# The last step of six layer norms moved from VectorE to ScalarE, in a two-layer decoder pipeline on one core

## The reference, cut to what matters

```
def _layernorm(x, axis=-1, eps=1e-05):
    m = jnp.mean(x, axis=axis, keepdims=True)
    v = jnp.var(x, axis=axis, keepdims=True)
    return (x - m) / jnp.sqrt(v + eps)

x = _layernorm(x + L0_attn(x))          # norm 1
x = _layernorm(x + L0_xattn(x, ctx))    # norm 2
x = _layernorm(x + L0_ffn(x))           # norm 3
x = _layernorm(x + L1_attn(x))          # norm 4, the scan
x = _layernorm(x + L1_xattn(x, ctx))    # norm 5
x = _layernorm(x + L1_ffn(x))           # norm 6, the experts
```

## Time and profile before

| | us |
|---|---|
| median of 3 runs | 3486.57 |
| lowest and highest | 3484.23, 3490.03 |
| the profiled execution's own time | 3486.94 |
| its span, first to last instruction | 3485.1 |
| TensorE matmuls busy | 2634.2 |
| VectorE busy | 2650.8 |
| ScalarE busy | 1564.4 |
| GpSimd busy | 1610.6 |

### The profile page before, as it was taken

How to read it: one execution, slowest core, us unless ns; L and a number is a source line. 1 busy time by engine, 2 the same in 40 slices (tenths; PEclk the granted TensorE clock), 3 DMA queues, 4 the chain that set the end, 5 groups by cost and what they waited for, 6 DMA issues and landing times.

```text
span 3485.1 us, 41835 instructions
## 1 busy us (share of the span) xinstructions
PE 2634.2 (76%) x10956; PEld 1505.0 (43%) x10956; DVE 2650.8 (76%) x4314; ACT 1564.4 (45%) x2838; POOL 1610.6 (46%) x1223
## 2 busy tenths in 40 slices
PE   5876878787786887768787786877778787777746
PEld 3434435354443544435354443544445353443413
DVE  2287887968789687887968789696877968788693
ACT  1364544535345453544535445453544545354430
POOL 1064461735537263562735437262562726447180
PEclk8868788887888878888887888888788887888877
DMA  3000000000000000000000000000000000000000
GB/s 115 0 16 0 21 1 27 0 22 6 0 27 0 27 0 7 21 0 27 0 22 6 0 27 0 27 0 13 15 0 27 0 22 6 0 12 0 12 0 12
DMA packets 16786, 45.63 MB, mean 13 GB/s; under 512 B 2376, under 2 KB 6992, under 8 KB 16336
## 3 DMA queue, kind: packets, MB, share of 16 engines
q1 hardware_dynamic: 16592, 43.90, 3.5%
HBM read 35.50 MB, written 8.39 MB: 13 GB/s over the span
## 4 chain that ended last, share of the span: by engine, by line
PE 37%; DVE 28%; issue 19%; ACT 9%; POOL 4%; DVEq 2%; SPq 0%; DMA 0%; ACTq 0%; POOLq 0%
PE bank L487 35%; DVE h_ring L1010 10%; POOL ysum L1537 4%; DVE x L392 3%; DVE x L1107 2%; PE bank L400 2%; DVE smax L915 2%; DVE soft L990 2%; ACT a_ring L1372 1%; DVE ln_stats L374 1%; DVE xpad L1016 1%; ACT soft L1349 1%; DVE qT L965 1%; ACT bank L1367 1%; ACT kmask L1312 1%
## 5 line engine op out<-in xcount | busy, mean ns | idle before, releaser
L1537 POOL TENSOR_TENSOR ysum<-ysum,h_ring 128x512 f32<-128x512 f32 x896 | 1152.4, 1286 | 476.5 <-DVE h_ring L1010 411.2
L1010 DVE TENSOR_TENSOR_SCAN h_ring<-a_ring,bank 128x512 f32<-128x512 f32 x1024 | 1170.9, 1199 | 103.2 <-ACT a_ring L1372 50.8
L487 PE MATMUL bank<-w_expert_w,x45T 128*128 128x512 f32 x1024 | 607.8, 732 | 226.2 <-DVE x L1107 224.6
L1372 ACT ACTIVATE a_ring<-soft,decay 128x510 f32<-128x510 f32 x1024 | 666.7, 715 | 141.7 <-DVE h_ring L1010 140.2
L1513 POOL TENSOR_TENSOR kmask<-kT,w_columns 128x960 f32<-128x960 f32 x64 | 115.5, 1838 | 753.8 <-ACT kT L1260 753.8
L487 PEld LDWEIGHTS bank<-w_expert_w,x45T 128*128 128x128 f32 x1024 | 212.3, 224 | 501.4 <-DVE x L1107 276.2
L1282 ACT ACTIVATE probs<-bank 120x512 f32<-120x512 f32 x256 | 138.3, 593 | 411.8 <-PE bank L487 411.8
L487 PE MATMUL bank<-kmask,w_cn_w 128*128 128x256 f32 (+2 forms) x768 | 277.3, 470 | 44.1 <-ACT kmask L1316 20.3
L400 PE MATMUL bank<-w_ident,x 128*128 128x128 f32 x640 | 136.8, 350 | 224.9 <-DVE x L392 224.9
L1107 DVE SCALAR_TENSOR_TENSOR x<-bank,weight,x 128x256 f32<-128x256 f32 x512 | 212.0, 471 | 72.0 <-PE bank L487 72.0
L962 DVE TENSOR_SCALAR kmask<-kmask,gate_scale,base 128x256 f32<-128x256 f32 x96 | 40.3, 420 | 278.7 <-ACT kmask L1326 278.7
(11 more groups left out here) (144 smaller groups left out, 3879.8 us busy)
## 6 DMA issues: line engine op xcount, KB each, us to landing
x0T<-in_xT SPq DMA_DIRECT2D x16, 512.0 KB, 3.2
x<-in_x SPq DMA_DIRECT2D x16, 512.0 KB, 4.2
out<-x SPq DMA_DIRECT2D x16, 512.0 KB, 3.1
ctxT<-in_ctxT SPq DMA_DIRECT2D x16, 240.0 KB, 4.3
ctxTb<-in_ctxT SPq DMA_DIRECT2D x16, 240.0 KB, 2.6
ctxb<-in_ctx SPq DMA_DIRECT2D x16, 240.0 KB, 3.1
w_expert_w<-in_expert_w SPq DMA_DIRECT2D x1, 2048.0 KB
w_winT<-in_winT SPq DMA_DIRECT2D x1, 1024.0 KB
```

What stands on the lines that cost most here:

```text
L487: return pe.matmul(o, l, r, start=start, stop=stop)
L1010: scanned.then(v.tensor_tensor_scan(h_ring[:, k % HRING, :], a_ring[:, k % RING, :, :].rearrange("p b s -> p (b s)"), xc2, 0.0, ALU.mult, ...
L1372: a.activation(a_ring[:, k % RING, :, 1:S], delta[:, c, :].rearrange("p (b s) -> p b s", b=NB)[:, :, 1:S], ACT.Exp, scale=decay[:, k:k + 1 ...
L1537: p.tensor_tensor(out=total, in0=first, in1=h_ring[:, k % HRING, :], op=ALU.add)\
```

## The change

The apply of all six norms becomes one ScalarE activation for each tile: Identity with scale rstd and bias shift, where shift = -mean x rstd. VectorE makes the shift of all four tiles in one instruction (`norm_shift`, 128x4) in the place where its applies stood, and signals it; ScalarE's four activations stand right behind the norm's rstd (`norm_apply`). For norm 6 VectorE's instruction moves from the end of the turn to between norm 4's and norm 3's sum. Tiles, transposes, copies and all other instructions stay.

```diff
--- before.py
+++ after.py
@@ -251,6 +251,7 @@
                 self.mv = sb(f"{name}_mv", [P, NT, 2])
                 self.logv = sb(f"{name}_logv", [P, NT])
                 self.rstd = sb(f"{name}_rstd", [P, NT])
+                self.shift = sb(f"{name}_shift", [P, NT])
                 self.x = x
                 self.sum = x if sum_ is None else sum_
                 self.xT = xT
@@ -259,6 +260,7 @@
                 self.var_ready = sem(f"{name}_var_ready", 1)
                 self.log_ready = sem(f"{name}_log_ready", 1)
                 self.rstd_ready = sem(f"{name}_rstd_ready", 1)
+                self.shift_ready = sem(f"{name}_shift_ready", 1)
                 self.x_ready = sem(f"{name}_x_ready", NT)
                 if xT is not None:
                     self.turned = sem(f"{name}_turned", DC)
@@ -386,11 +388,16 @@
             a.wait_ge(n.log_ready.sem, n.log_ready.at(g, 1))
             a.activation(n.rstd[:, :], n.logv[:, :], ACT.Exp, scale=-0.5).then_inc(n.rstd_ready.sem, 1)
 
-        def norm_apply(v, n, g):
+        def norm_shift(v, n, g):
             v.wait_ge(n.rstd_ready.sem, n.rstd_ready.at(g, 1))
+            v.scalar_tensor_tensor(out=n.shift[:, :], in0=n.mv[:, :, 0], scalar=-1.0, in1=n.rstd[:, :],
+                                   op0=ALU.mult, op1=ALU.mult).then_inc(n.shift_ready.sem, 1)
+
+        def norm_apply(a, n, g):
+            a.wait_ge(n.shift_ready.sem, n.shift_ready.at(g, 1))
             for t in range(NT):
-                v.tensor_scalar(n.x[:, t, :], n.sum[:, t, :], n.mv[:, t, 0:1], n.rstd[:, t:t + 1],
-                                ALU.subtract, ALU.mult).then_inc(n.x_ready.sem, 1)
+                a.activation(n.x[:, t, :], n.sum[:, t, :], ACT.Identity, bias=n.shift[:, t:t + 1],
+                             scale=n.rstd[:, t:t + 1]).then_inc(n.x_ready.sem, 1)
 
         def norm_turn(pe, n, g, banks):
 
@@ -1121,18 +1128,11 @@
                 last.then_inc(n.var_ready.sem, 1)
                 n.chain.end()
 
-            def ln6_apply(g):
-                n = n6
-                v.wait_ge(n.rstd_ready.sem, n.rstd_ready.at(g, 1))
-                for t in range(NT):
-                    v.tensor_scalar(n.x[:, t, :], acc[:, t, :], n.mv[:, t, 0:1], n.rstd[:, t:t + 1],
-                                    ALU.subtract, ALU.mult).then_inc(n.x_ready.sem, 1)
-
             def turn_(f, m, b):
 
                 if f is not None:
                     ln1_sum(f)
-                    norm_apply(v, n1, f)
+                    norm_shift(v, n1, f)
                 if b is not None:
                     gated(b)
                 if f is not None:
@@ -1144,7 +1144,7 @@
                 if f is not None:
                     maxima(f, 0, 2)
                 if b is not None:
-                    norm_apply(v, n5, b)
+                    norm_shift(v, n5, b)
                 states(m, 1)
                 if f is not None:
                     maxima(f, 2, 3)
@@ -1194,7 +1194,7 @@
                     ln2_sum(f)
                 states(m, 53)
                 if f is not None:
-                    norm_apply(v, n2, f)
+                    norm_shift(v, n2, f)
                 if b is not None:
                     combine(b, 12, 14)
                 states(m, 58)
@@ -1213,13 +1213,13 @@
                     if m is not None and s == CYC - 2:
                         ln4_sum(m)
                 if m is not None:
-                    norm_apply(v, n4, m)
+                    norm_shift(v, n4, m)
+                if b is not None:
+                    norm_shift(v, n6, b)
                 if f is not None:
                     ln3_sum(f)
                 if f is not None:
-                    norm_apply(v, n3, f)
-                if b is not None:
-                    ln6_apply(b)
+                    norm_shift(v, n3, f)
 
             scanned.n = None
             setup()
@@ -1398,10 +1398,12 @@
                     feat(f, 1)
                 if m is not None:
                     norm_rstd(a, n3, m)
+                    norm_apply(a, n3, m)
                 if b is not None:
                     norm_copy(a, n4, b, MB)
                 if f is not None:
                     norm_rstd(a, n1, f)
+                    norm_apply(a, n1, f)
                 if b is not None:
                     gated(b)
                 if m is not None:
@@ -1422,6 +1424,7 @@
                     softplus(m)
                 if b is not None:
                     norm_rstd(a, n5, b)
+                    norm_apply(a, n5, b)
                     norm_copy(a, n5, b, MB)
                 decays(m, 6)
                 if b is not None:
@@ -1441,6 +1444,7 @@
                 decays(m, 54)
                 if f is not None:
                     norm_rstd(a, n2, f)
+                    norm_apply(a, n2, f)
                 decays(m, 56)
                 if f is not None:
                     copy_and_sum(f)
@@ -1464,8 +1468,10 @@
                     nat()
                 if m is not None:
                     norm_rstd(a, n4, m)
+                    norm_apply(a, n4, m)
                 if b is not None:
                     norm_rstd(a, n6, b)
+                    norm_apply(a, n6, b)
 
             setup()
             turn_(0, None, None)
```

## The result

| | before | after |
|---|---|---|
| median of 4 runs each, us | 3485.40 (3482.41 to 3490.03) | 3546.23 (3540.93 to 3550.92) |
| ratio | | 1.0176, 95% interval 1.0163 to 1.0189 |
| span of the profiled execution, us | 3485.1 | 3539.1 |

The change makes the kernel slower by 1.8%: 61 us between the medians, 54 between the two profiled executions (the one of after is the shortest of its four). The forecast was 3518, 32 us slower, with a range up to 3552: the sign and the range hold, but the forecast size is little more than half of the measured one, and the forecast's own narrower range (3500 to 3540) misses it.

A forecast was written before the change was run, and what follows sets the result against it. No engine is full; waits between engines bound the kernel. Seam 13 x 3.43 less norm 5 and norm 2 14 x 1.84 gives +18.8 us, edges +13, together +32: 3518 us, own range 3500 to 3540, 8-in-10 range 3472 to 3552.

The forecast's parts named there:

- The rival of cheaper applies: All ScalarE applies: two per-partition operands cost as one, four applies take 1.70 us, kernel 3497; chance 0.10.
- The seam: Between two turns: norms 4, 6 and 1 on ScalarE delay the table load and TensorE by 3.43 us, 13 times.
- the norm-1 sum: VectorE behind its loop branch at the seam: first norm-1 sum starts 1.15 us later, because the resume stands bare.
- Norm 5: Within each turn: shift held by one GpSimd addition, then ScalarE applies; 1.76 us gained, bounds 2.6 and 0.5.
- Norm 2: Behind a VectorE scan: last output 1526.60 against 1526.68, so nothing; decays held up are hidden by four expert additions.
- Outside the loop: First turns, the turn behind the loop and the last one: norms' handoffs and applies add +13 us together.
- the sum: Whole loop: 13 seams of +3.43 us less 14 turns of 1.84 us make +18.8 us.
- Both clock rivals: TensorE's clock falls at the norm-3 projections (3563, chance 0.10) or returns early at norm 5 (3465, chance 0.14).
- The rival at the seam: Norm-3 projections: longer wait lowers TensorE's clock, about 3.5 us 13 times, +45 us, 3563; chance 0.10.
- a sign that the prediction named as wrong: TensorE: a granted clock that falls before the norm-3 projections would show the forecast wrong.
- The rival in which the clock makes it faster: Norm 5: transposes end 1.8 us sooner and 2.4 GHz returns at once, 3.8 us a turn, 3465; chance 0.14.
- C: Theory put to the follow-up runs: TensorE's granted clock decides what a turn keeps of a gain or loss.

The follow-up runs named there:

- the last kernel: Kernel before with norms 2 and 5 applied on ScalarE, plus 28 identity transposes and three more in each gap between norm 5's first four transposes: 3435.26 us.
- the fuller fillers: Kernel before with norm 5 on ScalarE, 28 identity transposes on TensorE and three more in each gap between norm 5's first four transposes: 3435.77 us.
- both delays: Kernel before with three, or thirteen, small ScalarE Identity instructions ahead of the gate's first Gelu in every turn: 3491.64 us and 3530.21 us.
- the changed kernel with fillers: Changed kernel with 28 identity transposes on TensorE ahead of norm 5's transposes: 3491.84 us, ratio 1.0017 to before.
- with more: Kernel before with 28 identity transposes and six more in each gap between norm 5's first four transposes: 3490.04 us, ratio 1.0013.

## Why the prediction was right, and where it was short

**The apply.** Estimated 591 ns and 2.04 us for four; the rows have 589 ns (x320 and x64) and 2.07. The estimate worked out from the Trainium skill (ScalarE: Activation LUTs, What ACT_TABLE_LOAD costs) was 2.06; with two pointer operands the trace now agrees. The rival of cheaper applies is out.

**The seam.** Forecast +3.43 us to the table load, measured +2.77. The features came as worked out (+3.9 for +4.1, the second's end +1.5 for +1.7), and so did norm 1's handoff and applies: from its second sum to the table load 3.11 us became 5.41, +2.30 for the forecast +2.28. The piece that was too large is the norm-1 sum, +0.5 for +1.15: VectorE's resume behind its branch took 2.75 to 2.99 us in the 13 seams of after (2.8 in the rows above), where the 13 of before have 3.29 to 3.52. The resume was carried over as a constant, and it isn't one. The applies in flight at the branch don't explain it: with norms 2 and 5 on ScalarE and the fillers, VectorE has the same eight applies ahead of its branch as before and its resume takes 2.77 to 3.12 us. The cause stays open.

**Norm 5.** Shift held by one GpSimd addition, applies on ScalarE: forecast 1.76 us gained, measured 2.77 - 0.92 = 1.85. **Norm 2:** nothing, forecast, and shown by the last kernel. **Outside the loop:** +7 us for a forecast +13.

**The step that failed is the sum** "13 x 3.43 - 14 x 1.84 = +18.8 us". Its terms were right within 0.7 us, and they make 2.77 - 1.85 = 0.92 us a turn, 12 us in 13 turns; the loop took 47. The other 2.7 us a turn have no term, because the sum lets a shift of 0.9 us go through the rest of the turn unchanged. That the first softmax came at the forecast place is luck: the sum had a shift of 1.67 us there from norm 5 on, and the runs 0.92 at norm 5's copies and 0.6 more lost to the clock behind them. The shift doesn't go through unchanged: the granted clock of TensorE falls and comes back at other places of the work. Both clock rivals looked for that at the spot of the edit (the norm-3 projections, norm 5's transposes). The rival at the seam does occur, and with it a sign that the prediction named as wrong, a clock that is low ahead of and in the norm-3 projections (10.1 to 13.5 and 23.8 to 27.2 us), but only in three of the eleven turns, in which the first projection comes at 23.7 us. The largest loss is in another place in most turns, at 92 to 103 us, 45 us behind norm 5's transposes, in the attention and expert matmuls, where no instruction was changed. That this is the clock and not the new operations is shown twice: 13 small instructions at the seam in the old kernel give the same windows there and 45 us, and 28 fillers on TensorE take the loop's loss away while all of the seam's delay stays. The measured 3546 lies in the range only because the range had been widened towards the clock cases and a dearer apply: the apply wasn't dearer, and the clock cost its time in another place than they had it.

**The rival in which the clock makes it faster** was priced at 3.8 us a turn and given 0.14. It didn't happen in this change, nor with norm 5 alone moved; but something like it can: with norm 5 alone moved and TensorE kept busy, the clock returns 3.4 us sooner and each turn is 3.4 us shorter.

**What stays open.** Why turns have lengths of about 204.8, 208.2, 211.6 and 215.0 us, within 0.7 us, in all fourteen kernels, isn't settled. The rows show this much: where the turns are alike, the clock changes at the same places of each (with norm 5 on ScalarE and the fuller fillers it is low from 54.8 to 71.8 and from 88.9 to 92.3 us in all eleven, to 0.1 us). C was right on the changed kernel without norm 5, on both delays, on the changed kernel with fillers (in kind) and on norm 5 with fillers, and wrong on norm 5 alone, on norm 1 back on VectorE and on the kernel before with 28 transposes and with more: which shift lands on which side of a step wasn't predictable from the rows.

## What to carry to other kernels

Where TensorE's granted clock goes up and down within each turn of a loop, the price of a small delay is not its size: 0.3 us cost between nothing and 3.4 us a turn here, and a gain of 2 us cost 14 us in all. Read the granted clock window by window over a whole turn, far behind the edit too, and keep a range of one such step a turn. Before a move is judged as bad, try it with TensorE kept busy in its longest wait: the same move can then pay. At its own place, a move off a busy engine gains where the moved work ran beside a competitor (norm 5 beside GpSimd, 4.83 us to 2.07) and costs where the receiving engine stands on the chain (norm 1 at the seam, 2.3 us); what the turn keeps of either is another matter.

## What the runs showed of the hardware

- Idle TensorE time isn't free: 28 transposes of 128x128 that compute nothing, 3.3 to 5.5 us in a turn, made the changed kernel 54 us faster (3546.23 to 3491.84) and the kernel before 3 us (3484.93 to 3481.62).
- A low-clock stretch can be shortened by 7 us a turn without any gain, if its end stays where it was (in the kernel before with 28 transposes: 51.4 to 75.3 us of the turn for 44.6 to 75.3).
- An Identity activation with both scale and bias per partition takes 589 ns for 128x256 from SBUF to SBUF, and four in a row 2.07 us; one of 128x1 takes 188 ns, and thirteen in a row 1.3 us, since each starts 93 ns behind the one before.
- A 128x4 VectorE operation on two SBUF tensors takes 0.14 to 0.16 us alone and 0.70 to 0.92 us where it starts while a GpSimd addition is running; each of the 47 such shifts in three of the kernels ended 0.02 us behind that addition.
- The engines' resume behind the loop branch took 2.4 to 2.7 us on ScalarE, 2.8 to 3.0 us (after), 3.3 to 3.5 us (before) and up to 3.7 us (norm 5 on ScalarE with 28 transposes) on VectorE, and 0.3 us on TensorE; on ScalarE in after it overlaps the applies that it has in flight when it branches (972.05 to 974.12, first record behind the branch at 974.5).
